# Combining the two exponentials of every second attention step on GpSimd instead of VectorE

## The reference

```python
A1 = jnp.einsum('bhqd,bhkd->bhqk', Q1, K1) * s
A2 = jnp.einsum('bhqd,bhkd->bhqk', Q2, K2) * s
P = jax.nn.softmax(A1, axis=-1) - lam * jax.nn.softmax(A2, axis=-1)
O = jnp.einsum('bhqk,bhkd->bhqd', P, V)
```

## Time and profile before

| | us |
|---|---|
| median of 3 runs | 1940.58 (1940.29 to 1941.86) |
| profiled execution | 1935.32 |
| its span, first to last instruction | 1933.5 |
| busy in the span: TensorE | 1856.4 (96%) |
| VectorE | 1512.5 (78%) |
| ScalarE | 1417.2 (73%) |
| GpSimd | 703.8 (36%) |

### The profile page before, as it was taken

How to read it: one execution, slowest core, us unless ns; L and a number is a source line. 1 busy time by engine, 2 the same in 40 slices (tenths; PEclk the granted TensorE clock), 3 DMA queues, 4 the chain that set the end, 5 groups by cost and what they waited for, 6 DMA issues and landing times. The chain is left out here.

```text
span 1933.5 us, 33239 instructions
## 1 busy us (share of the span) xinstructions
PE 1856.4 (96%) x10753; PEld 1442.1 (75%) x10753; DVE 1512.5 (78%) x2500; ACT 1417.2 (73%) x3298; POOL 703.8 (36%) x757
## 2 busy tenths in 40 slices
PE   5999999999999999999999999999999499999997
PEld 4866777777777777777777777777776399999896
DVE  5588888888888888888888888888888376666265
ACT  5588888888888888888888888888888376666100
POOL 2144333333333333333322333322223375555443
PEclk9799999999999999999999999999999799999999
DMA  8689888888888888888898888888885666666898
GB/s 290 181 219 258 212 221 224 225 223 234 225 222 225 225 228 228 207 231 227 220 232 230 225 222 227 222 228 227 220 212 137 241 208 238 234 236 212 285 385 285
DMA packets 228132, 446.09 MB, mean 231 GB/s; under 512 B 28962, under 2 KB 119888, under 8 KB 221968
## 3 DMA queue, kind: packets, MB, share of 16 engines
q1 hardware_dynamic: 223216, 434.02, 81.5%
q0 software_dynamic: 4768, 10.25, 1.8%
HBM read 184.34 MB, written 58.50 MB: 126 GB/s over the span
## 5 line engine op out<-in xcount | busy, mean ns | idle before, releaser
L536 ACT ACTIVATE e<-p_score,nmax 128x512 f32<-128x512 f32 x1024 | 695.4, 685 | 149.1 <-DVE nmax L743 145.5
L743 DVE TENSOR_REDUCE nmax<-p_score 128x2 f32<-128x1024 f32 x512 | 621.8, 1214 | 209.2 <-PE p_score L850 205.3
L386 POOL TENSOR_SCALAR e<-e,rrec,lam 128x512 f32<-128x512 f32 x512 | 394.6, 771 | 971.0 <-DVE rrec L708 971.0
L850 PE MATMUL p_score<-ks,qs 128*128 128x512 f32 x2048 | 580.3, 405 | 3.4 <-ACT e L536 3.3
L850 PEld LDWEIGHTS p_score<-ks,qs 128*128 128x128 f32 x2048 | 366.2, 189 | 177.6 <-issue 101.7
L815 PE MATMUL p_proj<-xh,w 128*128 128x512 f32 x1024 | 386.6, 418 | 5.8 <-POOL xl L370 3.7
L715 DVE SCALAR_TENSOR_TENSOR pm<-e,rrec 128x512 f32<-128x512 f32 x512 | 385.3, 753 | 0.7 <-POOL e L386 0.7
L470 ACT COPY pT<-p_tr 128x512 f32<-128x512 f32 x512 | 301.1, 588 | 96.8 <-PE p_tr L860 89.1
L860 PEld LDWEIGHTS p_tr<-consts,pm 128*128 128x128 f32 x2048 | 248.9, 140 | 88.5 <-issue 27.4
L860 PE MATMUL p_tr<-consts,pm 128*128 128x128 f32 x2048 | 308.5, 273 | 4.3 <-ACT pT L470 4.3
L875 PE MATMUL p_pv<-pT,v 128*64 128x512 f32 x1024 | 247.7, 605 | 2.0 <-DVE oT L720 2.0
(11 more groups left out here) (141 smaller groups left out, 1895.8 us busy)
## 6 DMA issues: line engine op xcount, KB each, us to landing
ks<-k_parts SPq DMA_DIRECT2D x512, 256.0 KB, 4.4
qs<-q_parts SPq DMA_DIRECT2D x512, 128.0 KB, 2.7
w<-weight_parts_scratch SPq DMA_DIRECT2D x56, 1024.0 KB, 9.3
w<-in_w SPq DMA_DIRECT2D x46, 1024.0 KB, 7.2
oT_scratch<-oT SPq DMA_DIRECT2D x64, 512.0 KB
op<-oT_scratch SPq DMA_DIRECT2D x32, 1024.0 KB
wv<-weight_parts_scratch SPq DMA_DIRECT2D x56, 256.0 KB, 7.9
weight_parts_scratch<-w SPq DMA_DIRECT2D x8, 1024.0 KB
```

The lines of the kernel that those rows point to most:

```text
L386: nc.gpsimd.tensor_scalar(e2, e2, rrec[:, g % 4, 1:2], lam[:, 0:1], ALU.mult, ALU.mult).then_inc(s_e2, 1)
L536: nc.scalar.activation(ex[:, g % EX, m, :], p_score[g % 2][:, m, :], ACT.Exp, bias=nmax[:, g % 2, m:m + 1], accum_out=rsum[:, g % 4, m:m + ...
L743: vec.tensor_reduce(nmax[:, g % 2, :], p_score[g % 2][:, :, :], AXX, ALU.max, negate=True).then_inc(s_max, 1)
L850: last_op = nc.tensor.matmul(p_score[g % 2][:, m, :], qs[j][u][:, m, qt * P:(qt + 1) * P], ks[j][u][:, m, part, :], start=(part == 0), sto ...
```

## The change

In odd steps GpSimd, behind its scaling of the second exponential, also scales the first one by its reciprocal, in place, waits for both results and for the transposes of g - 4, and adds the two into pm. It signals that on a semaphore of its own, s_padd. VectorE calls `combine` for even steps only. Whoever waited for s_comb now waits, through `combined(g)`, for s_comb or s_padd by the parity of the step. Step 511, the last, is odd.

```diff
--- before.py
+++ after.py
@@ -170,7 +170,8 @@
         s_xhi, s_xlo = sem("a_xhi"), sem("a_xlo")
         s_proj, s_hi, s_lo, s_vp, s_v = sem("a_proj"), sem("a_hi"), sem("a_lo"), sem("a_vp"), sem("a_v")
         s_score, s_max, s_exp = sem("a_score"), sem("a_max"), sem("a_exp")
-        s_rec, s_e2, s_comb = sem("a_rec"), sem("a_e2"), sem("a_comb")
+        s_rec, s_e2, s_e1 = sem("a_rec"), sem("a_e2"), sem("a_e1")
+        s_comb, s_padd = sem("a_comb"), sem("a_padd")
         s_tr, s_pT, s_pv, s_ohi, s_olo = sem("a_tr"), sem("a_pT"), sem("a_pv"), sem("a_ohi"), sem("a_olo")
         s_ost = [sem(f"a_ost{j}") for j in range(2)]
         s_scat, s_lam, s_bq = sem("a_scat"), sem("a_lam"), sem("a_bq")
@@ -189,6 +190,10 @@
         AT_STEP = {0: "q0", 1: "k0", 2: "q1", 3: "k1"}
         V_STEP = 6
         PV_STEP = {5: (0, 1), 7: (2, 3)}
+
+        def combined(g):
+
+            return (s_comb if g % 2 == 0 else s_padd), g // 2 + 1
 
         def batch_of(pair):
             return pair // PAIRS
@@ -384,6 +389,14 @@
                 if g == 0:
                     pool.wait_ge(s_lam, 1)
                 nc.gpsimd.tensor_scalar(e2, e2, rrec[:, g % 4, 1:2], lam[:, 0:1], ALU.mult, ALU.mult).then_inc(s_e2, 1)
+                if st % 2 == 1:
+                    e1 = ex[:, g % EX, 0, :]
+                    nc.gpsimd.tensor_scalar(e1, e1, rrec[:, g % 4, 0:1], None, ALU.mult).then_inc(s_e1, 1)
+                    pool.wait_ge(s_e2, g + 1)
+                    pool.wait_ge(s_e1, g // 2 + 1)
+                    if g >= 4:
+                        pool.wait_ge(s_tr, g - 3)
+                    nc.gpsimd.tensor_tensor(pm[:, g % 4, :], e1, e2, ALU.add).then_inc(s_padd, 1)
                 if pair + 3 < PAIRS:
                     if st == 2:
                         low_v(pair + 3)
@@ -532,7 +545,7 @@
                             act.wait_ge(s_wvlo, 3)
                             act.wait_ge(s_wqlo, 6)
                         if g >= EX:
-                            act.wait_ge(s_comb, g - EX + 1)
+                            act.wait_ge(*combined(g - EX))
                     nc.scalar.activation(ex[:, g % EX, m, :], p_score[g % 2][:, m, :], ACT.Exp,
                                          bias=nmax[:, g % 2, m:m + 1],
                                          accum_out=rsum[:, g % 4, m:m + 1]).then_inc(s_exp, 1)
@@ -745,7 +758,7 @@
                 what = AT_STEP.get(st - 1)
                 if what and pair + 1 < NPAIRS:
                     low_part(pair + 1, what)
-                if g >= 2:
+                if g >= 2 and st % 2 == 0:
                     combine(g - 2)
                 if g in (FIRST_V, FIRST_V + 1):
                     add_bv(g - FIRST_V)
@@ -759,7 +772,6 @@
             for g in range(STEPS - 2, STEPS):
                 reciprocals(g)
             combine(STEPS - 2)
-            combine(STEPS - 1)
             low_o(NPAIRS - 2)
             low_o(NPAIRS - 1)
 
@@ -853,7 +865,7 @@
                 last_op.then_inc(s_score, 1)
 
             def transposes(g):
-                pe.wait_ge(s_comb, g + 1)
+                pe.wait_ge(*combined(g))
                 if g >= 1:
                     pe.wait_ge(s_pT, g)
                 for k in range(QT):
```

## The result

The changed kernel takes 2005.08 us (median of 4 runs, 1999.97 to 2008.53) against 1940.65 for the kernel before in the same comparison: 1.0329 times as long, interval 1.0303 to 1.0355. The forecast was 1932.7, faster; it is 64 us slower, far outside the range. The profiled execution took 2008.53 us with a span of 2006.7, 73.2 us more than the profiled execution before.

A forecast was written before the change was run, and what follows sets the result against it. TensorE bounds attention, with a stall of 0.07 or 0.22 us per pair that VectorE's lateness passes on through ScalarE. Minus 7.7, minus 1.5, plus 1.3 is minus 7.9 us: 1940.58 to 1932.7 us, range 1929.5 to 1940.

The forecast's parts named there:

- costing of GpSimd's group: GpSimd in odd steps: two scalings of 0.77 us, a 0.09 us wait and a 1.28 us addition, together 2.9 us.
- the term for the start: First pairs: one odd combination leaves VectorE ahead of each of TensorE's two waits, twice 0.75, minus 1.5 us.
- The addition: GpSimd's sum of two 128x512 operands: 1.28 us; 1.5 us by the skill page's ratio, still within 0.8 us of slack.
- GpSimd is late: Rival, chance 0.08: step 1's transposes and the waiting combination; slower once the group exceeds 2.9 us by over 0.8 us.
- The queue behind the group: Next even scaling stands behind GpSimd's three; VectorE's even combination waits, some 0.3 us at step 6, hidden by idle time.
- The steady gain: 57 pairs: TensorE's stalls go, 25 times 0.22 us and 32 times 0.07 us, minus 7.7 us; at best 9.5.
- The signs that it named for the steady pairs: Pairs 22.08 to 22.11 us, transposes 1.37 to 1.40 apart, step 3's reduction within 0.05 of scores' end, group 2.9.
- the 0.32 us by which VectorE was late: Step 3's reduction starts 0.32 us after the scores' end, put down to a combination taking 0.89 us instead of 0.75.
- Collisions: Program order keeps GpSimd's group off VectorE's combinations; they meet only at the very end; nothing counted elsewhere.
- No DMA is moved: Whole kernel: semaphores and the moved loop test cost nothing and no DMA is moved; nothing counted.
- The end: Last, odd step: GpSimd's three cost 0 to 2.9 us; plus 1.3 us taken, 0.77 scaling ahead and 0.53 collision.
- TensorE is full: Rival, chance 0.12: attention's middle, TensorE busy 200 of 200 us, so nothing is gained; about 1941.9 us.

The follow-up runs named there:

- the fast form: The changed kernel with the first exponential scaled by two factors (its reciprocal and a column of ones) in all odd steps: 1943.25 us, ratio 1.0000.
- The opened ring: The changed kernel, slow scaling kept, with VectorE issuing odd reciprocals one step earlier, ahead of the even combination: 1950.53 us, ratio 1.0050.
- the run whose end is as before: The changed kernel, slow scaling kept, but with GpSimd's odd-step sums only in the first five pairs: 1956.94 us, ratio 1.0074.

## Why the prediction was wrong

**The step that failed** is in the costing of GpSimd's group: "The scaling of the first exponential has the shape of the one there, 0.77 us". The tile has the shape, but the old instruction does two operations and the new one does one, and the one takes 1.56 us. The group is 3.7 us instead of 2.9. A price was taken from a row that is alike in tile and engine and differs in the form of the operation, and no bounds were set round it, though the trace had no row of the new form. This step alone doesn't mend the forecast: with the assumed 0.77 us made true, the kernel takes 1943.25 us, still above the range, because the term for the start failed too (below). The Trainium skill, GPSIMD Engine Reference, Engine selection, gives no warning of it: it has elementwise work with one input roughly at line rate on GpSimd. The trace disagrees for the form with one operation, 1.56 us where the form with two takes 0.77. The addition, for which the prediction weighed that section, was right: 1.288 us, 1.71 times VectorE's 0.753 and less than the factor of about 2 there.

**The rival "GpSimd is late"** is what came, and its point was well placed. It was to decide 0.8 us beyond 2.9; the runs give the ring as the exact form: a pair needs four turns and 0.60 us, TensorE 22.08, so a turn may last 5.37 us. With the fast form a turn is shorter than the slow form's 5.50 by the 0.79 us between the two scalings, 4.71, and that is what its last pair shows (GpSimd's scalings that begin a turn at 1491.92 and 1496.63); 0.66 us are left. The slow form is 0.13 over, four times a pair. Its chance of 0.08 rested on the sentence that no row of this size was over 1.34 us, and that was the same failed step.

**The queue behind the group** was seen in half: the prediction had the even combination wait, "some 0.3 us", hidden by VectorE's idle time. It missed that the odd reciprocal, which starts GpSimd's next group, stands behind that combination. What it took for one short wait is a closed ring, and idle time on VectorE can't hide a ring that runs through VectorE. The opened ring shows it: 1.0050 for 1.0329 with the same slow scaling.

**The steady gain** was right: minus 7.7 us forecast for the 57 pairs, 9.2 less in the trace of the fast form (its best end was 9.5), 7.1 less in the medians where the first five pairs and the last are left as they were. The signs that it named for the steady pairs came with the fast form: pairs of 22.08 of both kinds, transposes 1.37 us apart, a group of 2.95 us, the reduction of step 3 within 0.05 us of the scores' end. One reading on the way was loose: of the 0.32 us by which VectorE was late, the stretched combination (0.89 for 0.75) is 0.14; the rest is its unbroken work before, and in pairs without the split it was late by some 0.17.

**Collisions** were rightly excluded by program order. The run with the earlier reciprocals gives that order up and shows the price: its scaling that meets a combination takes 1.19 us for 0.77.

**"No DMA is moved"** failed: none changes place in the code, but one in time. SyncE's store waits for a GpSimd instruction that the group pushed back, and a load stands behind it. Where the forecast had minus 1.5 us at the start, the first five pairs lost 17.6 us: 8.6 of them go with the fast form, another 7.9 once the subtraction goes first, and 1.1 stay. The gain itself was put too high: TensorE's two waits of 4.11 and 1.95 us are 4.53 and 1.94 in the changed kernel, and 3.94 and 1.34 with the fast form.

**The end**: plus 1.3 us forecast, 8.5 measured to the start of the last product. With the fast form it is 2.3, and 0.7 in the run whose end is as before, so that for the assumed group the forecast was near. The collision that it named came (the slow scaling of the last step takes 1.99 us for 1.56), and the place was right; with the slow form the size was far too small, because in the last pair TensorE has no projections and would be quicker than the ring, so that every step waits for it and not only the last (its turns there are 5.51 us, GpSimd's scalings that begin them at 1557.09 and 1562.60).

**TensorE is full** fell as argued from the starts of the pairs. The row was 200 of 200 us busy; the fast form, with pairs shorter by 0.16 us, shows 200 of 200 as well:

```profile
700.00:900.00 200.00, 200.00 (x1051) 145.23 (x1050) 153.30 (x236) 168.27 (x408) 142.65 (x164) 1.00 0.90 228
```

The warning of the Trainium skill, Trainium Kernel Development and Optimization, Best Practices, that matmul busy share is not how the distance from the roofline is judged, agrees with these two rows.

What stays open: the last pair was not changed alone in any run, so its share is from the traces; what the lower granted clock costs in the first pairs; and why the form with one operation is slow, which was not looked into.

## What to carry to other kernels

Take the price of a new instruction only from a row that agrees in engine, tile and form (number of operations, where the factors come from); where there is none, bound it from both sides, or measure it alone first. Before work is moved into another engine's queue, write down the ring: who issues what the moved work waits for, and does that stand, in program order, behind something that waits for the moved work; its length against the bound of the stage decides, and an instruction issued earlier can open it. Then look at what else stands behind the moved work in that queue and at the DMA queues that wait for it: one subtraction in the wrong place cost 8 us here.

## What the hardware showed that was not expected

On GpSimd a TENSOR_SCALAR of 128x512 f32 takes 0.77 us with two operations and two columns of factors, 1.56 us with one operation and one column, and 1.49 us with one operation and a constant. Doing more is quicker: the column of ones is worth 0.79 us per instruction.
